# A fused two-attention transformer block on one core: a new work order in the iterations that project slices, and a rebuilt hand-over between the attentions

## The reference, cut to what matters

```python
x = x + attn_a(layernorm(x))   # x: 2 x 2048 x 256, 16 heads of 16, softmax over all 2048 keys
x = x + ffn(layernorm(x))      # relu(x W_fc)^2 W_proj, then a 5-step spiking neuron, count / 5
x = x + attn_b(layernorm(x))
x = x + ffn(layernorm(x))      # the same weights again

# attn_a: att = softmax(q k^T / 4); opt[b,l,h,:] = sum_m att[b,l,m,h] * v[b,l,h,:], then W_out, b_out
# attn_b: q, k, v = (x W + b).reshape(b, 16, 16, 2048)
#         attn = softmax(k^T v * temperature); out = q attn^T
# neuron, five times: reset = mem > 1; mem = 0.9 mem + y - reset; count += mem > 1
```

## Time and profile before

| | |
|---|---|
| median of 3 runs | 2655.95 us (2655.7 to 2658.02) |
| the profiled execution | 2661.87 us |
| its span, first to last instruction | 2660.1 us |
| mean granted TensorE clock | 0.976 |
| busy PE / DVE / ACT / POOL | 2305.4 / 2494.0 / 2529.3 / 1282.6 us |
| scores and exponentials | 1024 chunks in attention a, 1024 in attention b |

### The profile page before, as it was taken

One profiled execution on the slowest core, in us unless ns is written; L12 is line 12 of the kernel. 1 busy time (PEld: TensorE's weight loads), 2 busy tenths in 40 slices (PEclk: granted clock), 3 DMA queues, 4 the chain that ended last, 5 costly groups with the idle time before them and its releaser, 6 DMA issues. The chain is left out here.

```text
span 2660.1 us, 39493 instructions
## 1 busy us (share of the span) xinstructions
PE 2305.4 (87%) x12443; PEld 1069.9 (40%) x12672; DVE 2494.0 (94%) x3274; ACT 2529.3 (95%) x4763; POOL 1282.6 (48%) x1891
## 2 busy tenths in 40 slices
PE   5788888878788878878878999999999999999998
PEld 2244444434334334433433334444343434343434
DVE  4799999999999999999998999999999999999995
ACT  4799999999999999999998999999999999999994
POOL 0146666655455555545543244444444444444444
PEclk8799999999999999999999999999999999999999
DMA  6612222233410111111111111111111111111110
GB/s 210 135 38 70 62 64 65 57 79 74 99 44 23 43 44 31 35 44 36 30 58 38 57 38 38 48 45 36 42 48 45 32 46 46 42 34 48 45 30 17
DMA packets 190936, 140.82 MB, mean 53 GB/s; under 512 B 92164, under 2 KB 177670, under 8 KB 190727
## 3 DMA queue, kind: packets, MB, share of 16 engines
q1 hardware_dynamic: 190406, 137.69, 18.7%
q10 hardware_dynamic: 320, 0.59, 0.1%
HBM read 92.04 MB, written 41.94 MB: 50 GB/s over the span
## 5 line engine op out<-in xcount | busy, mean ns | idle before, releaser
L1081 DVE TENSOR_REDUCE nmax<-score 128x1 f32<-128x1024 f32 x1024 | 1200.1, 1215 | 80.2 <-PE score L840 70.2
L1333 ACT ACTIVATE score<-score,nmax 128x1024 f32<-128x1024 f32 x1024 | 1122.2, 1105 | 42.1 <-DVE nmax L1081 39.6
L840 PE MATMUL score<-big,shared 128*128 128x512 bf16 x1956 | 622.6, 400 | 245.4 <-ACT score L1333 204.9
L1050 DVE TENSOR_SCALAR_CACHE_REDUCE big<-score 128x1024 f32<-128x1024 f32 x672 | 787.6, 1215 | 10.6 <-PE score L777 7.9
L1287 ACT ACTIVATE big<-big,nmax 128x1024 f32<-128x1024 f32 x672 | 766.4, 1145 | 5.8 <-DVE big L1050 4.1
L777 PE MATMUL score<-shared 128*128 128x512 bf16 x1911 | 532.2, 382 | 61.1 <-ACT big L1287 39.0
L758 PE MATMUL bank_g<-big,qw 128*32 128x512 f32 x4096 | 493.8, 600 | 1.0 <-ACT qcol L1316 1.0
L1053 DVE TENSOR_REDUCE nmax<-score 128x1 f32<-128x1024 f32 x352 | 414.8, 1216 | 20.7 <-PE score L777 19.7
L1287 ACT ACTIVATE big<-score,nmax 128x1024 f32<-128x1024 f32 x352 | 389.3, 1112 | 6.7 <-DVE nmax L1053 6.7
L840 PEld LDWEIGHTS score<-big,shared 128*128 128x128 bf16 x2048 | 133.2, 98 | 562.2 <-ACT score L1333 489.0
L777 PEld LDWEIGHTS score<-shared 128*128 128x128 bf16 x2048 | 161.7, 98 | 425.3 <-ACT big L1287 169.5
(11 more groups left out here) (150 smaller groups left out, 1880.7 us busy)
## 6 DMA issues: line engine op xcount, KB each, us to landing
shared<-q_parts SPq DMA_DIRECT2D x256, 64.0 KB, 2.4
shared<-kb_parts SPq DMA_DIRECT2D x256, 64.0 KB, 2.2
shared<-vb_parts SPq DMA_DIRECT2D x256, 64.0 KB, 2.2
big<-k_parts SPq DMA_DIRECT2D x48, 192.0 KB, 5.2
big<-k_parts SPq DMA_DIRECT2D x24, 256.0 KB, 7.9
kb_parts<-pieces SPq DMA_DIRECT2D x96, 64.0 KB, 1.6
vb_parts<-pieces SPq DMA_DIRECT2D x96, 64.0 KB, 1.6
shared<-in_x SPq DMA_DIRECT2D x32, 128.0 KB, 2.4
```

The lines of the kernel that those rows point to most:

```text
L840: last = mm(score_a(turn, c)[:, k * BANK:(k + 1) * BANK], qstack[:, par, c // NCH, :], keys[:, b, c // NCH, col:col + BANK], start=True, s ...
L1050: v.tensor_scalar(row_chunk(c), score_b(turn, c)[:, :], -1.0, INF, ALU.mult, ALU.min, accum_out=nmax[:, par, c // NCH, c % NCH:c % NCH + 1 ...
L1081: v.tensor_reduce(nmax[:, par, c // NCH, c % NCH:c % NCH + 1], score_a(turn, c)[:, :], AX.X, ALU.max, negate=True).then_inc(max_a, 1)
L1333: a.activation(s[:, :], s[:, :], ACT.Exp, bias=nmax[:, par, c // NCH, c % NCH:c % NCH + 1], accum_out=esum[:, par, c // NCH, c % NCH:c % N ...
```

## The change

Three things change. First, iterations 3 to 10 use a new table, `LATE`, and the slices' own places become tables: PE's v passes stand behind chunks 3 and 5 (before 4 and 5), its k and q passes behind 4, 6, 8, 9 (before 3, 6, 8, 9), ACT takes the slice's q behind chunk 9 (before 8), and DVE's slice statistics and normalisations are each split over two chunks. Second, the left-over projections in iterations 33 and 34 use a table `LEFT`. Third, the hand-over: head 0's query column gets a semaphore of its own, `first_q`, waited for by POOL alone; the first eight products of head group 0 move from iteration 32 (behind chunks 22 to 31) to iteration 33 (`CARRIED`, behind chunks 0 to 4), with DVE's staging in iteration 33 waiting for them one by one; POOL's weighting work in iteration 32 is spread out and later; and tile 31's neuron moves from DVE (`last_neuron`, behind chunk 8 of iteration 33) to POOL.

```diff
+LEFT = dict(turn_x2=9, kv=[11, 12, 14, 17], q=[19, 20], take_x2=7, take_k=15, take_v=16, take_q=[19, 20],
+            stats_x2=0, mean_x2=1)
 BESIDE = dict(turn_opt=9, out=[10, 11], turn_x2=12, kv=[13, 14, 15, 16], q=[18, 20],
...
+LATE = dict(turn_opt=7, out=[10, 10], turn_x2=12, kv=[13, 13, 14, 15], q=[20, 22],
...
+SLICE_EARLY = dict(stats=[14, 14], mean=16, norm=[25, 25])
+SLICE_LATE = dict(stats=[12, 16], mean=18, norm=[23, 24])
+SLICE_V, SLICE_KQ, TAKE_SLICE_Q = [3, 5], [4, 6, 8, 9], 9
...
+CARRIED = [0, 0, 1, 1, 3, 3, 4, 4]
...
         def plan(it):
 
+            if NE - 1 <= it < N_STEPS:
+                return LATE
             return ALONE if N_STEPS <= it < T - 1 else BESIDE
...
-            return isinstance(n, int) and n in (T - 1, 2 * T - 2, 2 * T - 1)
+            return isinstance(n, int) and n in (2 * T - 2, 2 * T - 1)
...
-                    load_b_q(0, 0)
+                    sp.dma_start(qcol[:, 0, :], qb_cols[0:P, :]).then_inc(first_q, 16)
...
-                    if isinstance(i, int):
-                        pe.wait_ge(b_loaded[par], 16 * 17 * (i // 2 + 1))
-                    else:
-                        pe.wait_ge(b_loaded[par], 8 * 17 * (i - par) + 16 * 17)
+                    pe.wait_ge(b_loaded[par], 16 * 17 * (i // 2 + 1) - 16 * (1 - par))
...
-                    if head0(it):
-                        head_product(0, c)
...
+                    for n, at_c in enumerate(CARRIED):
+                        if i1 == 0 and c == at_c:
+                            product(0, 0, n)
...
-                if c % (CPT // 4) == 0:
+                if i == 1 and c < CPT // 2:
+                    if c % NCH == 0:
+                        dve.wait_ge(prod_done, c // NCH + 1)
+                elif c % (CPT // 4) == 0:
                     need(dve, prod_done, H * (i - 1) + (c // (CPT // 4) + 1) * (H // 4))
...
-                if c == 18:
+                if c == (25 if i == 0 else 18):
                     row_rec(i, 0)
...
-                        if left_over(it) == T - 2 and c == 8:
-                            dve.wait_ge(qkv_xn, T - 2)
-                            last_neuron(T - 1, par, 0, x2_stored[par], 8 * (T - 1 - par))
...
-                if c == 15:
+                if c == (21 if i == 0 else 15):
                     row_fac(i, 0)
...
+                if n == 0:
+                    pool.wait_ge(first_q, 16)
                 pool.wait_ge(w_rec, n + 1)
...
+                if i3 is not None:
+                    split_kv(i3)
                 if head0(it):
                     half_distance(0, 0, 0)
-                    half_sums(0, 0, 0)
-                    weigh_q(0, 0, 0)
-                if i3 is not None:
-                    split_kv(i3)
...
+                if head0(it):
+                    half_sums(0, 0, 0)
...
                 if i1 is not None:
                     square(i1, 1)
+                if head0(it):
+                    weigh_q(0, 0, 0)
...
+                if it == 1:
+                    pool.wait_ge(qkv_xn, T - 2)
+                    result(T - 1, T - 1, par, x2_stored[par], 8 * (T - 1 - par))
```

More of the change, by code:

```diff
@@ L75 @@
               rec=4, add=11, stats_x1=12, mean_x1=13, stats_x2=6, mean_x2=7)
+LATE = dict(turn_opt=7, out=[10, 10], turn_x2=12, kv=[13, 13, 14, 15], q=[20, 22],
+            turn_x1=17, up=[18, 19, 19, 21, 23, 23, 23, 24], down=[26, 27, 27, 28, 29, 29, 30, 30],
+            fac=0, take_opt=7, take_x2=10, take_x1=15, take_k=14, take_v=16,
+            take_q=[22, 24], relu=[20, 23], take_y=29,
+            rec=4, add=10, stats_x1=11, mean_x1=12, stats_x2=0, mean_x2=6)
+SLICE_EARLY = dict(stats=[14, 14], mean=16, norm=[25, 25])
+SLICE_LATE = dict(stats=[12, 16], mean=18, norm=[23, 24])
+SLICE_V, SLICE_KQ, TAKE_SLICE_Q = [3, 5], [4, 6, 8, 9], 9
 ALONE = dict(turn_opt=7, out=[8, 9], turn_x2=10, kv=[12, 13, 15, 15], q=[17, 19],
@@ L293, in build @@
         b_loaded = [sem(f"b_loaded{r}") for r in range(2)]
+        first_q = sem("first_q")
         x2_loaded = sem("x2_loaded")
@@ L783, in head_product @@
                 for n, at_c in enumerate(PROD_AT[1]):
-                    if c == (min(at_c, CPT - 1) if isinstance(i, int) and i == 0 else at_c):
+                    if c == at_c:
                         product(i, 0, n)
@@ L1108, in phase_a @@
                     if ahead is not None:
-                        if c == 14:
-                            slice_stats(ahead)
-                        if c == 16:
+                        at_s = SLICE_LATE if u is not None else SLICE_EARLY
+                        for s in range(SLS):
+                            if c == at_s["stats"][s]:
+                                slice_stats(ahead, s)
+                        if c == at_s["mean"]:
                             slice_aggr(ahead)
-                        if c == 25:
-                            slice_norm(ahead)
+                        for s in range(SLS):
+                            if c == at_s["norm"][s]:
+                                slice_norm(ahead, s)
             iterations(phase_a)
@@ L1605, in phase_b @@
                 n, f = tile_at(it, LIF_LAG), tile_at(it, FFN_LAG)
+                n_tile = T - 1 if it == 1 else T + it - LIF_LAG
                 def count(first, last):
-                    if n is not None:
-                        spikes(T + n, T - 1 + n, par, first, last)
+                    if n is not None or it == 1:
+                        spikes(n_tile, n_tile, par, first, last)
                 i3 = left_over(it)
```

47 lines of the change are left out of this document (24 added, 23 removed).

## The result

The changed kernel takes 2626.57 us (median of four runs, 2625.46 to 2628.29) against 2656.98 us for the kernel before beside it (four runs, 2655.7 to 2661.33). The ratio is 0.9889 with a 95% interval of 0.9877 to 0.9901: 29.5 us less, 26 to 33. The forecast was 2632 us, 23.6 to 24 less, in a range of 2622 to 2646. Faster was right, the time is inside the range, and it lies 5.4 us under the number, 0.6 us from the 2626 of the case called "more than forecast".

What follows compares the result with a forecast made beforehand. ACT (95% busy) and DVE (94%) were taken as nearly full, so only idle time could be won. Slices 17.1 us plus hand-over 6.5 made 23.6, from a median of 2655.95 to 2632 us, range 2622 to 2646.

Steps and rivals of the forecast that it cites:

- more than forecast: Rival: slices gain 2.7 us each, as the chunk walk says, and the hand-over 10; 2626 us, chance 0.06.
- The three waits of the slices: ACT waits in iteration 6: 0.68 us for `opt` transposes, 0.58 behind paired statistics, 0.72 behind paired normalisations.
- (1): Slices: `turn_x2` on PE must wait for ACT's later q read-out; a margin of about 0.6 us.
- (2): Slices: small DVE operations and first slice statistics meet behind chunks 10 to 12; 0.2 to 0.3 us allowed.
- (3): Slices: three FFN up passes together behind chunk 23 take PE 1.3 us and delay score 24; nothing to 0.2 us.
- (a): Hand-over: PE no longer waits for the query column at attention b's first scores; ACT gains 1.71 us.
- (b): Hand-over: `fac` moves from behind chunk 15 to 21 and no longer waits for POOL; 1.10 us gained.
- (c): Hand-over: without products in iteration 32, 4.65 us of waits go and a relu wait of 0.4 returns; 4.25 gained.
- x2 read-out: Hand-over: its 1.62 us ACT wait followed a low-clock stretch; half, 0.8 us, taken as gone.
- (d): Iteration 33: neuron moved from DVE to POOL regains 2.48 us of ACT waiting, plus 1.3 of slow PE behind it.
- (e): Iteration 33: carried products make ACT 4.7 us late by score 7, plus 1.2 behind chunks 12 to 15; cost 5.9.
- the fifth rival: The clock falls in the slice iterations, 4.6 us late in each; slower, 2669 us, chance 0.05.

Runs made afterwards that it cites:

- opt_late: The changed kernel with the `opt` transposes behind chunk 9 again in iterations 3 to 10; a single execution took 2633.26 us.
- dve_pairs: The changed kernel with DVE's slice statistics together behind chunk 14 and both normalisations behind 25 again; a single execution took 2632.32 us.
- q_waited: The changed kernel with PE's first scores of attention b waiting for the query column's transfer again; a single execution took 2630.50 us.
- products_back: The changed kernel with the eight products in iteration 32 again, and the old order of `fac` and POOL there; a single execution took 2631.11 us.
- left_old: The changed kernel with the old table `BESIDE` for the left-over projections; iteration 34 took 39.49 us against 40.26.
- slices_only: The kernel before with only the slices' edits, the hand-over as before; 2633.37 us against 2656.32, ratio 0.9911.
- neuron_back: The changed kernel with the last neuron of attention a on DVE again, behind chunk 8 of iteration 33; a single execution took 2632.75 us.

## Why the prediction was right, and where its sizes were off

*What bounds the kernel.* Right: ACT, and the slices had more to give than the hand-over. The limit was not: 17.1 us of ACT idleness was called the most that the slices could give, and they gave 21.5.

*The three waits of the slices.* Right in their causes (opt_late, dve_pairs), and all three are gone. Of the new waits the text allowed for, (1) had a margin of 0.36 us, (2) shows no wait, (3) shows none. **The term that was mis-sized is the 2.3 us per iteration**: it was 2.88, in iteration 10 1.42 and not 1.0, together 21.5 us and not 17.1. The prediction's own terms (2.0 removed, 0.4 added, 0.3 and 0.3 for overlap and small waits) make 2.2; of the 0.7 missing, 0.4 are the new waits, of which none came, and 0.3 the overlap. The text stopped at 41.65 us, "which is what ACT is busy for". But busy time was not fixed: with the waits gone, ACT is busy for 41.09 us and not 41.66, since a wait leaves an accumulator read or a short read-out standing alone that otherwise lies under the next instruction. The text counted 0.3 us for that; it is 0.57. (With one wait back, in opt_late, ACT is busy for 41.14 us, with two, in dve_pairs, for 41.26.) The walk over the 32 chunks gave 41.2, and was put aside as short by some tenths; it was right to 0.1 us. (In new wait (3), twelve matmuls of 128 columns at half of 1.03 us for four are 1.5 us, not 1.3. No wait came of it.)

*The hand-over.* Its sum, 6.5 us, agrees with the 7.2 measured alone and the 5.9 that it adds to the slices, but by errors that cancel, which is luck:

| term | forecast | the runs |
|---|---|---|
| (a) query column | 1.71 | 1.2 to 1.3 (q_waited) |
| (b) and (c) `fac`, product waits | 1.10 + 4.25 | 6.0 (products_back) |
| x2 read-out | 0.8 | 0 to 1.6, by the clock's stretch |
| (d) neuron | 2.48 + 1.3 | 3.4, or 1.9 with the products carried |
| (e) carried products | -5.9 | -3.1 |
| `LEFT` | +0.6 | -0.8 |

With (d) taken at 3.4 and x2 at nothing, the right-hand column sums to 6.7 to 6.8. **Two steps failed.** (e): PE's 13.1 us from score 0 to score 7 were right (13.0). Up to there the products cost 3.6 us and not 4.7, because PE was about 1.0 us ahead at score 0 and not 0.4, and ACT needs 8.4 us for these chunks without the carried products (products_back) and not 8.0. The 1.2 us charged at chunks 12 to 15 were no cost of theirs at all, since that wait stands there without them. With the products back, iteration 33 still has 1.36 us of ACT idleness, and the carried products raise it to 4.31, by 2.95 us and not by the sum of the waits. `LEFT`: the sign was wrong. The sum counted its earlier statistics and transposes and put its earlier k and v passes at nothing; by the rows of left_old the statistics bring 0.88 us in iteration 33, and the passes take 0.77 there and 0.79 in iteration 34, by making PE's score late. With their other waits and overlaps the two tables differ by 0.04 us in length in iteration 33 and by 0.77 in iteration 34. The x2 read-out's 0.8 us was neither right nor wrong: the wait depends on the clock's stretch, not on the change.

*The signs named for the changed profile.* Iterations 3 to 9 are 41.1 us, under the 41.4 to 42.0 given, with ACT idle for 0.00 and DVE for 1.1. No transfer releases PE at attention b's first score, iteration 32 is under 44 us, and iteration 33 has 4.8 us of ACT idleness by the windows of the earlier trace rows (43.23 - 38.42; 4.3 from exponential to exponential), most before chunk 8, just under the 5 to 6 given. The granted clock is 1.00 in iterations 3 to 10 and in 33, so the fifth rival did not happen; PE's busy share there rose to 87% and 94%. The prediction took the slow matmuls at 1373.48 as following from 2.06 us of idleness; q_waited has 1.99 us of it at the same place and the six matmuls run at 2.4 GHz, so that wait alone does not bring the low clock.

*The rest.* 3.8 us of the two profiled spans lie ahead of iteration 3, where neither half changes the work. In the execution of before the clock is at 1.2 GHz from 90.1 to 114.0 us and again from 154.9 to 158.3, in the first one of the changed kernel only from 91.1 to 101.4. Seven of the other versions, slices_only and neuron_back among them, look like before there (at 1.2 GHz until 112.6 to 114.2 us), though their code for that part is the changed kernel's, so it is no property of the change. The slices' 23.6 us as timed and 21.5 by profile differ by a remainder that may be of this kind and lies inside the interval.
